# Regrouping the softmax denominator matmuls and double-buffering the sign staging of a binarized weight, in a fused attention and linear kernel

## The chip, the cores and the metric

The kernel runs on the 8 cores of one Trainium2 chip. Each core computes one element of the batch of 8, with its own copy of all weights, and no core talks to another. The metric is the device time in microseconds of the slowest core; the profile is that of the slowest core of one profiled execution. A comparison of two kernels here tells about 2% from no change.

## What is computed

Per batch element, with x of 2048 x 2048 in float32, 16 heads of size 128:

```
def _L0_attn_ref(x, W_Q, W_K, W_V, W_O, b_Q, b_K, b_V, b_O):
    q = einsum('bpd,hde->bphe', x, W_Q) + b_Q          # k, v likewise
    scores = einsum('bqhe,bkhe->bhqk', q, k) / ATTN_SCALE
    scores = where(causal, scores, IGNORE)
    attn = softmax(scores, axis=-1)
    z = einsum('bkhe,bhqk->bqhe', v, attn)
    return einsum('bqhe,hed->bqd', z, W_O) + b_O

def _L0_ffn_ref(x, weight, bias):
    alpha = mean(abs(weight), axis=1, keepdims=True)
    bw = where(weight >= 0, 1.0, -1.0) * alpha
    return einsum('bsi,oi->bso', x, bw) + bias

x = x + _layernorm(_L0_attn_ref(_layernorm(x), ...))
x = x + _layernorm(_L0_ffn_ref(_layernorm(x), weight, bias))
```

## The kernel before, in words

The program is written out by hand for five engines. `p.op(engine, ..., wait=[...], inc=...)` appends one instruction to that engine's list, with the semaphore counts it waits for. Each engine runs its own list strictly in order, so an instruction that waits holds up all that stands behind it in the same list. DMAs are issued from the lists of `sync` (SP) and `gpsimd` (POOL). Nothing is scheduled by a tool: the order of the Python calls is the order on each engine.

There are three stages.

1. First layernorm and transposes of x into `arena_a`, with the projections of head 0 (to about 220 us of the span).
2. The 16 heads, about 130 us each. Per head: the K projection (`emit_w_mms`, 64 matmuls of 512 columns into psD, psE, psC), the V projection (64, into psA and psB), a bound on the scores (`emit_mh_sq`, `emit_mh_mms`, `emit_mh_tail`, `emit_mb`) that becomes `mbias`, and 16 transposes of V. Then come four query groups g = 0 to 3 of 512 queries. Group g has 4(g+1) key chunks of 128 keys. The Q projection of the next head (64 matmuls, psA and psB) is issued behind the last group's denominators.
3. The binarized weight is made (`emit_bw_tile`, 16 tiles of 128 rows), and then 16 row tiles of x run through the output projection (`emit_front_pe`, L759), layernorm, transposes and the second linear layer (L868), and the last layernorm.

**One query group.** For each key chunk j, TensorE makes the scores transposed (`emit_score`, L569, one matmul of 512 columns) in one of four PSUM halves: chunks 0, 1 in psA, 2, 3 in psB, 4, 5 in psA again, and so on. ScalarE turns a pair of chunks into exponentials with one instruction over 1024 columns (`emit_exp`, L583), written to `ptil`. A score matmul waits until the exponential that last read its half is done. The last four chunks of a group stand on the causal diagonal: POOL zeroes the part left of it (L593) and multiplies the diagonal block with a triangle (L596), both in `emit_mask`. The denominators (`emit_den`, L608) are matmuls of an all-ones matrix with each chunk, summed in psC. A denominator matmul waits for the chunk's exponential, or for its mask. Then ScalarE computes the reciprocal as Ln (L637) and Exp (L641), VectorE multiplies every chunk by it (L651), and TensorE multiplies with V (L669) into psE. The scores of the first four chunks of the next group are issued before these L669 matmuls; their exponentials overwrite `ptil` and wait for L669 to have read it.

**What sets the order.** In the kernel before, `emit_emd` emits for each pair an exponential, the masks, and the two denominator matmuls; only then are the next two scores emitted:

```
for j in range(min(4, nchunks), nchunks):
    emit_score(g + 1, j, pe_sc)
    if (j + 1) % estep == 0 and j + 1 > 4:
        emit_emd(g + 1, j + 1 - estep, pe_sc, sc_exp, gp_mask_j)
```

**The binarized weight.** For tile t: POOL loads 128 rows of the weight (L408, 1 MB, two buffers `fwst`), VectorE sums the absolute values (L411) and scales the sum (L415), ScalarE writes the sign into `v_sb` (L421), VectorE multiplies by alpha (L425), TensorE transposes 16 blocks into psD and psE (L438), ScalarE copies both into `arena_a` (L444). There is one staging buffer, `v_sb`, so the sign of tile t+1 waits for the transposes of tile t; it also stands behind the copies of tile t in ScalarE's list. After tile 4, `emit_front_pe(0)` puts the first output projection on TensorE. `emit_front_pe(i)` first issues, from SP, the load of the attention output z of row tile i (L741, 512 KB, into `qt_sb` for even i and `kt_sb` for odd i) and of the x rows (L747).

Of the kernel before, what the change touches and what calls it, by code (L numbers as in the profile page):

```python
# [10 lines left out]
ALU = mybir.AluOpType  # L11
# [49 lines left out]
def build_program(SEQ, DM, H):  # L61
# [252 lines left out]
    pe_bw_last = 0  # L314

# [84 lines left out]

    def emit_bw_tile(t):
        nonlocal pe_bw_last
        fpar = t % 2
        wait = [("SC", sc_ln1t_all),
# [13 lines left out]
        w2 = [(FWs[fpar], fw_t), ("PE", pe_bw_last)]  # L418
        if t == 0:
            w2.append(("PE", pe_av_all[H - 1]))  # L420
        sc_sign_d[t] = p.op("scalar", lambda e, fpar=fpar: e.activation(  # L421
            v_sb[:], fwst[fpar], AF.Sign, bias=0.0, scale=1.0),
            wait=w2, inc="SC",
            lowp="binarized weight is a bf16 matmul operand")
        dv_bw = p.op("vector", lambda e: e.tensor_scalar(  # L425
            v_sb[:], v_sb[:], twoal[:, 0:1], None, ALU.mult),
# [3 lines left out]
        for half in range(2 if NCH > 1 else 1):  # L430
# [5 lines left out]
            for c in range(c0, c1):  # L436
                w3 = wait if c == c0 else ()
                tgt = p.op("tensor", lambda e, c=c, b=b, c0=c0: e.transpose(  # L438
                    b[:, (c - c0) * 128:(c - c0 + 1) * 128],
                    v_sb[:, c * 128:(c + 1) * 128],  # L440
                    eye_sb[:]), wait=w3, inc="PE" if c == c1 - 1 else None)
            pe_bw_last = tgt
            sc_bw_evac_half[half] = p.op(
                "scalar", lambda e, t=t, b=b, c0=c0, c1=c1: e.copy(  # L444
                    bwt3[:, c0:c1, t * 128:(t + 1) * 128],
                    b[:, 0:(c1 - c0) * 128].rearrange("p (c q) -> p c q",
                                                      c=c1 - c0)),
                wait=[("PE", pe_bw_last)], inc="SC")
# [72 lines left out]
    for h in range(H):  # L521
# [68 lines left out]
        def emit_mask(g, j, sc_exp, gp_mask_j):  # L590
            r = j - g * TPG
            if r > 0:
                p.op("gpsimd", lambda e, j=j, r=r: e.memset(  # L593
                    ptil[:, j * GQ:j * GQ + r * 128], 0.0),
                    wait=[("SC", sc_exp[j])], inc="GP")
            gp_mask_j[j] = p.op("gpsimd", lambda e, j=j, r=r: e.tensor_tensor(  # L596
                ptil[:, j * GQ + r * 128:j * GQ + (r + 1) * 128],
                ptil[:, j * GQ + r * 128:j * GQ + (r + 1) * 128],
                tri_sb[:], ALU.mult), wait=[("SC", sc_exp[j])], inc="GP")

        def emit_den(g, j, sc_exp, gp_mask_j):
            chunks = (g + 1) * TPG
            wait = [("SC", sc_exp[j])] if j < g * TPG else \
                [("GP", gp_mask_j[j])]
            if j == 0:
                wait.append(("SC", sc_rinv_prev))
            pe_den_d[g] = p.op("tensor", lambda e, j=j, chunks=chunks:
                               e.matmul(psC[:, 512:512 + GQ], onem_sb[:],  # L608
                                        pslot[j], start=(j == 0),
                                        stop=(j == chunks - 1)),  # L610
                               wait=wait,
                               inc="PE" if j == chunks - 1 else None)

        def emit_emd(g, j0, pe_sc, sc_exp, gp_mask_j):
            emit_exp(g, j0, pe_sc, sc_exp)
            for jj in range(j0, j0 + estep):
                if jj >= g * TPG:
                    emit_mask(g, jj, sc_exp, gp_mask_j)
                emit_den(g, jj, sc_exp, gp_mask_j)
# [383 lines left out]
```

How the kernel before makes its waits and increments, by code:

```python
        def thunk(e, fn=fn, wait=wait, inc=inc, incn=incn, lowp=lowp):  # L43
            for (s, v) in wait:
                e.wait_ge(sems[s][0], v)
            if lowp is not None:
                with nc.allow_low_precision(reason=lowp):
                    ins = fn(e)
            else:
                ins = fn(e)
            if inc is not None:
                ins.then_inc(sems[inc][0], incn)
```

## Time and profile before

| | us |
|---|---|
| median of 3 runs | 2859.36 |
| lowest and highest of these | 2858.36, 3082.75 |
| the profiled execution | 2857.58 |
| its span on the slowest core (core 7) | 2856.1 |
| spans of the 8 cores | 2848.7 to 2856.1 |
| mean granted TensorE clock of the cores | 0.806 to 0.810 of full speed |

The span runs from the first to the last instruction of a core; the profiled execution's time is 1.5 us longer. Engines are PE (TensorE matmuls), PEld (its weight loads), DVE (VectorE), ACT (ScalarE), POOL (GpSimd), and SP, which issues DMAs. A row of the timeline gives a start, a duration, engine, line, output and inputs, and in brackets how long the engine had sat idle before and what ended that.

### The profile page before, as it was taken

The page shows a single profiled execution, that of the slowest core. Times are in us where ns is not written, and L with a number is a line of the kernel's source. Part 1 is how long each engine was busy: PE and PEld are TensorE (multiplying, and loading weights), DVE is VectorE, ACT ScalarE, POOL GpSimd, SP SyncE. Part 2 cuts the span into 40 slices and gives each one's busy share as a digit, 9 for nine tenths or more (in the row PEclk, how much of TensorE's full clock was granted, in tenths as well). Part 3 has the DMA queues.
Part 4 walks back from the last instruction along what each step waited for, and adds up shares of the span by engine and source line. Part 5 has one row for each costly group of instructions (what it writes and reads, how often), then busy time and mean ns, then how long its engine had stood idle before and what let it go on. Part 6 is the DMA issues. An engine that isn't in the chain of part 4 may idle for free.

```text
span 2856.1 us, 27277 instructions; the slowest of 8 cores (2848.7 to 2856.1 us)
## 1 busy us (share of the span) xinstructions
PE 2027.9 (71%) x8336; PEld 827.4 (29%) x8336; DVE 937.5 (33%) x1696; ACT 629.9 (22%) x785; POOL 239.3 (8%) x558
## 2 busy tenths in 40 slices
PE   2556776858586776768586766768585549999995
PEld 1222222313132322323131322223131224444442
DVE  3432322223132222222232322222231445555554
ACT  1222122130303122121303121221303451111111
POOL 0001001010101000110101011011101000000000
PEclk9667877878686878778686878778786669999998
DMA  6410110202021110102021113122110522223221
GB/s 142 125 17 12 19 21 12 26 6 25 6 24 13 19 21 12 19 11 26 6 24 14 19 13 49 19 41 28 34 32 6 187 103 74 74 74 106 79 74 59
DMA packets 178474, 119.33 MB, mean 42 GB/s; under 512 B 168100, under 2 KB 168100, under 8 KB 170148
## 3 DMA queue, kind: packets, MB, share of 16 engines
q0 software_dynamic: 107200, 75.51, 14.6%
q1 hardware_dynamic: 71140, 42.07, 5.8%
q8 instruction: 79, 1.29, 0.2%
q14 instruction: 55, 0.45, 0.1%
HBM read 125.97 MB, written 25.17 MB: 53 GB/s over the span
## 4 chain that ended last, share of the span: by engine, by line
PE 62%; ACT 14%; issue 8%; DVE 8%; POOL 4%; DMA 2%; DVEq 1%; ACTq 1%; POOLq 0%
ACT ptil L583 10%; PE psA L362 8%; PE psB L362 8%; PE psC L608 7%; PE psE L669 5%; PE psC L362 4%; PE psA L759 4%; PE psC L868 4%; PE psB L759 4%; PE psB L569 3%; PE psA L569 3%; POOL ptil L596 2%; PE psD L868 2%; PE psE L868 2%; DVE ptil L651 2%
## 5 line engine op out<-in xcount | busy, mean ns | idle before, releaser
L608 PE MATMUL psC<-ptil,onem_sb 128*128 128x512 bf16 x640 | 274.2, 491 | 459.9 <-ACT ptil L583 165.3
L651 DVE TENSOR_TENSOR ptil<-ptil,c 128x512 bf16<-128x512 bf16 x640 | 220.4, 421 | 918.7 <-ACT c L641 918.7
L362 PE MATMUL psA<-arena_a,wbuf 128*128 128x512 bf16 x1024 | 319.7, 400 | 3.1 <-ACT arena_a L276 3.1
L362 PE MATMUL psB<-arena_a,wbuf 128*128 128x512 bf16 x1024 | 318.5, 399 | 2.8 <-ACT arena_a L276 2.8
L608 PEld LDWEIGHTS psC<-ptil,onem_sb 128*128 128x128 bf16 x640 | 63.9, 100 | 687.0 <-issue 675.8
L583 ACT ACTIVATE ptil<-psA,mbias 128x1024 bf16<-128x1024 f32 x160 | 178.1, 1113 | 343.4 <-PE psA L569 181.1
L583 ACT ACTIVATE ptil<-psB,mbias 128x1024 bf16<-128x1024 f32 x160 | 177.8, 1111 | 254.8 <-PE psB L569 254.8
L669 PE MATMUL psE<-ptil,v 128*128 128x512 bf16 x640 | 189.0, 430 | 28.6 <-DVE ptil L651 28.6
L596 POOL TENSOR_TENSOR ptil<-ptil,tri_sb 128x128 bf16<-128x128 bf16 x256 | 108.5, 424 | 1145.9 <-ACT ptil L583 1145.8
L487 ACT ACTIVATE srow<-srow 1x1 f32<-1x1 f32 x32 | 6.5, 202 | 843.9 <-DVE srow L482 843.9
L868 PE MATMUL psC<-arena_a,c 128*128 128x512 bf16 x512 | 153.1, 381 | 17.3 <-DVE c L852 17.3
L569 PE MATMUL psA<-qt,kt 128*128 128x512 bf16 x320 | 143.0, 542 | 27.1 <-DVE v L557 27.1
L362 PE MATMUL psC<-arena_a,wbuf 128*128 128x512 bf16 x544 | 157.2, 379 | 4.5 <-DVE qt L376 4.5
L569 PE MATMUL psB<-qt,kt 128*128 128x512 bf16 x320 | 147.2, 556 | 0.0
L362 PEld LDWEIGHTS psB<-arena_a,wbuf 128*128 128x128 bf16 x1024 | 104.7, 102 | 137.5 <-issue 28.9
L362 PEld LDWEIGHTS psA<-arena_a,wbuf 128*128 128x128 bf16 x1024 | 104.0, 102 | 139.5 <-issue 31.1
L669 PEld LDWEIGHTS psE<-ptil,v 128*128 128x128 bf16 x640 | 64.3, 101 | 176.2 <-issue 140.9
L868 PE MATMUL psD<-arena_a,c 128*128 128x512 bf16 x256 | 97.5, 381 | 0.0
L868 PE MATMUL psE<-arena_a,c 128*128 128x512 bf16 x256 | 97.3, 380 | 0.0
L362 PE MATMUL psD<-arena_a,wbuf 128*128 128x512 bf16 x240 | 90.9, 379 | 4.3 <-issue 3.4
L362 PE MATMUL psE<-arena_a,wbuf 128*128 128x512 bf16 x240 | 90.9, 379 | 0.0
L759 PE MATMUL psA<-arena_b,kt 128*128 128x512 bf16 x256 | 77.1, 383 | 3.4 <-ACT c L782 3.4
(124 smaller groups left out, 2082.4 us busy)
## 6 DMA issues: line engine op xcount, KB each, us to landing
c<-fw POOLq DMA_DIRECT2D x16, 1024.0 KB, 6.4
ptil<-x SPq DMA_DIRECT2D x16, 1024.0 KB, 6.9
out<-wbuf POOLq DMA_DIRECT2D x16, 1024.0 KB, 9.4
wbuf<-wq POOLq DMA_DIRECT2D x16, 512.0 KB, 6.4
wbuf<-wk POOLq DMA_DIRECT2D x16, 512.0 KB, 6.3
c<-x SPq DMA_DIRECT2D x8, 1024.0 KB, 5.9
wbuf<-wv POOLq DMA_DIRECT2D x16, 512.0 KB, 6.3
zs<-c SPq DMA_DIRECT2D x64, 128.0 KB, 2.0
```

The source lines that it names most:

```text
L362: e.matmul(banks[bidx], wslot[sl][:, c * 128:(c + 1) * 128], ln1t3[:, c, s * SLW:(s + 1) * SLW], start=(c == 0), stop=(c == NCH - 1)),
L487: t_ln = p.op("scalar", lambda e, wh=which: e.activation(srow[0:1, 18 + wh:19 + wh], srow[0:1, 16 + wh:17 + wh], AF.Ln, bias=0.0, scale=1. ...
L569: pe_sc[j] = p.op("tensor", lambda e, j=j, g=g, hb=hb: e.matmul(schalf[hb], kt_sb[:, j * 128:(j + 1) * 128], qt_sb[:, g * GQ:(g + 1) * GQ] ...
L583: t_exp = p.op("scalar", lambda e, buf=buf, dst=dst: e.activation(dst, buf, AF.Exp, bias=mbias[:, 0:1], scale=C_ATTN), wait=wait, inc="SC")
L596: gp_mask_j[j] = p.op("gpsimd", lambda e, j=j, r=r: e.tensor_tensor(ptil[:, j * GQ + r * 128:j * GQ + (r + 1) * 128], ptil[:, j * GQ + r * ...
L608: e.matmul(psC[:, 512:512 + GQ], onem_sb[:], pslot[j], start=(j == 0), stop=(j == chunks - 1)),
L651: dv_norm[j] = p.op("vector", lambda e, j=j, g=g: e.tensor_tensor(pslot[j], pslot[j], rbc[g % 2], ALU.mult), wait=wait, inc="DV")
L669: pe_av = p.op("tensor", lambda e, j=j, chunks=chunks: e.matmul(psE[:, 0:GQ], v_sb[:, j * 128:(j + 1) * 128], pslot[j], start=(j == 0), st ...
L759: p.op("tensor", lambda e, hh=hh, s=s, d=zrd: e.matmul(projb[s], d[:, hh * 128:(hh + 1) * 128], Bz[:, hh * DM + s * 512:hh * DM + s * 512 ...
L868: p.op("tensor", lambda e, c=c, s=s: e.matmul(ffnb[s], ln3t[:, c * 128:(c + 1) * 128], bwt3[:, c, s * 512:s * 512 + PSW], start=(c == 0), ...
```

## The change

It has two parts.

**Denominators and masks.** `emit_mask`, `emit_den` and `emit_emd` are gone. The loop over a group's pairs emits only scores and exponentials. At the head of the loop body for group g, all four masks are emitted, then all 4(g+1) denominator matmuls in a row, and then Ln and Exp as before. The number of instructions stays the same. POOL's and ScalarE's lists keep their order in this stage; only TensorE's changes.

```
-                emit_emd(0, j + 1 - estep, pe_sc, sc_exp, gp_mask_j)
+                emit_exp(0, j + 1 - estep, pe_sc, sc_exp)
         for g in range(NG):
             chunks = (g + 1) * TPG
-            pe_den = pe_den_d[g]
+            gp_mask_j = {}
+            for r in range(TPG):
+                j = g * TPG + r
...
+            pe_den = 0
+            for j in range(chunks):
+                wait = [("SC", sc_exp[j])] if j < g * TPG else \
+                    [("GP", gp_mask_j[j])]
+                if j == 0:
+                    wait.append(("SC", sc_rinv_prev))
+                pe_den = p.op("tensor", lambda e, j=j, chunks=chunks: e.matmul(
+                    psC[:, 512:512 + GQ], onem_sb[:], pslot[j],
+                    start=(j == 0), stop=(j == chunks - 1)),
+                    wait=wait, inc="PE" if j == chunks - 1 else None)
             p.drain("scalar")
...
                 for j0 in range(0, min(4, nchunks), estep):
-                    emit_emd(g + 1, j0, pe_sc, sc_exp, gp_mask_j)
+                    emit_exp(g + 1, j0, pe_sc, sc_exp)
                 for j in range(min(4, nchunks), nchunks):
                     emit_score(g + 1, j, pe_sc)
                     if (j + 1) % estep == 0 and j + 1 > 4:
-                        emit_emd(g + 1, j + 1 - estep, pe_sc, sc_exp,
-                                 gp_mask_j)
+                        emit_exp(g + 1, j + 1 - estep, pe_sc, sc_exp)
```

TensorE's list of the kernel before from the L669 matmuls of group 0 to those of group 1 (psA and psB take scores, psC denominators, psE the product with V):

```order
L669 MATMUL psE<-ptil,v 128x512 x4
L608 MATMUL psC<-ptil,onem_sb 128x512 x4
L569 MATMUL psA<-qt,kt 128x512 x2
L608 MATMUL psC<-ptil,onem_sb 128x512 x2
L569 MATMUL psB<-qt,kt 128x512 x2
L608 MATMUL psC<-ptil,onem_sb 128x512 x2
L569 MATMUL psA<-qt,kt 128x512 x2
L569 MATMUL psB<-qt,kt 128x512 x2
L669 MATMUL psE<-ptil,v 128x512 x8
```

The same stretch of the changed kernel, whose lines are L585 for scores, L635 for denominators and L672 for the product with V:

```order
L672 MATMUL psE<-ptil,v 128x512 x4
L585 MATMUL psA<-qt,kt 128x512 x2
L585 MATMUL psB<-qt,kt 128x512 x2
L635 MATMUL psC<-ptil,onem_sb 128x512 x8
L585 MATMUL psA<-qt,kt 128x512 x2
L585 MATMUL psB<-qt,kt 128x512 x2
L672 MATMUL psE<-ptil,v 128x512 x8
```

The eight denominators of group 1, which stood as four, two and two ahead of and between the score pairs, now stand in one block behind all of the group's scores. In groups 2 and 3 the block has 12 and 16.

**Binarized weight.** The sign goes to `v_sb` for even tiles and to `kt_sb` for odd ones, and waits for the transposes two tiles back. The copies out of psD and psE are emitted by a function of their own, `emit_bw_evacs`, behind the sign of the next tile.

```
+        stg = (v_sb, kt_sb)[fpar]
...
-        w2 = [(FWs[fpar], fw_t), ("PE", pe_bw_last)]
-        if t == 0:
+        w2 = [(FWs[fpar], fw_t), ("PE", pe_bw_par[fpar])]
+        if t < 2:
             w2.append(("PE", pe_av_all[H - 1]))
...
+        if t >= 1:
+            emit_bw_evacs(t - 1)
...
+        if i == 1:
+            wait.append(("PE", B_PE))
```

The last two lines are in `emit_front_pe`: since `kt_sb` now stages signs, the z load of row tile 1 waits for `B_PE`, the count of TensorE at the end of the transposes of tile 15. Behind it in SP's list stand the load of x rows 1 and the z load of row tile 2.

ScalarE's list of the kernel before at the start of the binarized weight (v and kt are the staging buffers, c holds the weight rows):

```order
L421 ACTIVATE v<-c 128x2048
L444 COPY arena_a<-psD 128x8x128
L444 COPY arena_a<-psE 128x8x128
L421 ACTIVATE v<-c 128x2048
L444 COPY arena_a<-psD 128x8x128
L444 COPY arena_a<-psE 128x8x128
```

And of the changed kernel, where L438 is the sign and L410 the copy:

```order
L438 ACTIVATE v<-c 128x2048
L438 ACTIVATE kt<-c 128x2048
L410 COPY arena_a<-psD 128x8x128
L410 COPY arena_a<-psE 128x8x128
L438 ACTIVATE v<-c 128x2048
L410 COPY arena_a<-psD 128x8x128
L410 COPY arena_a<-psE 128x8x128
L438 ACTIVATE kt<-c 128x2048
```

The sign of tile 1 now stands ahead of the copies of tile 0, and so on to the end, where the copies of tile 15 stand alone.

## Rows read from the trace of the kernel before

**Rows 1.** Page: the chain that ended last, share of the span by line

```profile
ACT ptil L583 10%; PE psA L362 8%; PE psB L362 8%; PE psC L608 7%; PE psE L669 5%; PE psC L362 4%; PE psA L759 4%; PE psC L868 4%; PE psB L759 4%; PE psB L569 3%; PE psA L569 3%; POOL ptil L596 2%; PE psD L868 2%; PE psE L868 2%; DVE ptil L651 2%
```

**Rows 2.** Groups of instructions: count | busy us, mean ns | idle before, releasers

```profile
L608 PE MATMUL psC<-ptil,onem_sb 128*128 128x512 bf16 x640 | 274.2, 491 | 459.9 <-ACT ptil L583 165.3 <-POOL ptil L596 158.8 <-POOL ptil L593 135.8
L583 ACT ACTIVATE ptil<-psA,mbias 128x1024 bf16<-128x1024 f32 x160 | 178.1, 1113 | 343.4 <-PE psA L569 181.1 <-DVE mbias L517 69.0 <-DVE ptil L651 58.7
```

**Rows 3.** Timeline of one head, groups 0 to 2: exponentials and one denominator row

```profile
1107.45 1.11 ACT L583 ACTIVATE ptil<-psA,mbias 128x1024 bf16<-128x1024 f32 x1 [4.30 <-DVE mbias L517]
...
1111.46 1.11 ACT L583 ACTIVATE ptil<-psB,mbias 128x1024 bf16<-128x1024 f32 x1 [2.89 <-PE psB L569]
...
1118.21 1.11 ACT L583 ACTIVATE ptil<-psA,mbias 128x1024 bf16<-128x1024 f32 x1 [1.96 <-PE psE L669]
...
1119.22 1.11 ACT L583 ACTIVATE ptil<-psB,mbias 128x1024 bf16<-128x1024 f32 x1
...
1125.07 1.11 ACT L583 ACTIVATE ptil<-psB,mbias 128x1024 bf16<-128x1024 f32 x1 [2.26 <-PE psB L569]
...
1133.19 0.59 PE L608 MATMUL psC<-ptil,onem_sb 128*128 128x512 bf16 x2
...
1145.14 1.11 ACT L583 ACTIVATE ptil<-psB,mbias 128x1024 bf16<-128x1024 f32 x1 [2.89 <-PE psB L569]
```

**Rows 4.** Timeline of the same head, group 3, to the next projection (L362)

```profile
1154.63 1.02 PE L608 MATMUL psC<-ptil,onem_sb 128*128 128x512 bf16 x4
...
1155.49 0.59 PE L569 MATMUL psA<-qt,kt 128*128 128x512 bf16 x2
...
1156.30 1.11 ACT L583 ACTIVATE ptil<-psA,mbias 128x1024 bf16<-128x1024 f32 x1 [2.29 <-PE psA L569]
...
1157.55 0.59 PE L608 MATMUL psC<-ptil,onem_sb 128*128 128x512 bf16 x2 [1.47 <-ACT ptil L583]
...
1160.85 1.06 PE L569 MATMUL psA<-qt,kt 128*128 128x512 bf16 x2
...
1162.12 1.11 ACT L583 ACTIVATE ptil<-psA,mbias 128x1024 bf16<-128x1024 f32 x1 [2.22 <-PE psA L569]
...
1172.78 1.11 ACT L583 ACTIVATE ptil<-psB,mbias 128x1024 bf16<-128x1024 f32 x1 [2.89 <-PE psB L569]
...
1175.02 0.42 POOL L596 TENSOR_TENSOR ptil<-ptil,tri_sb 128x128 bf16<-128x128 bf16 x1
...
1176.14 1.01 PE L362 MATMUL psA<-arena_a,wbuf 128*128 128x512 bf16 x2
```

**Rows 5.** Windows: stretch, length, busy us (count) by engine, granted clock, DMA share, GB/s

```profile
1118.20:1125.00 6.80, 3.22 (x12) 0.95 (x10) 0.69 (x1) 3.23 (x3) 0.95 (x3) 1.00 0.08 19
...
1159.10:1176.00 16.90, 8.56 (x18) 2.20 (x18) 0.00 (x0) 5.25 (x5) 2.95 (x8) 0.50 0.00 0
...
2345.00:2800.00 455.00, 445.73 (x2205) 201.58 (x2204) 249.40 (x362) 82.79 (x160) 7.46 (x14) 1.00 0.28 80
```

**Rows 6.** Timeline of the binarized weight and of the hand-over to row tile 1

```profile
2271.63 1.01 ACT L444 COPY arena_a<-psD 128x1024 bf16<-128x1024 bf16 x1 [14.51 <-PE psD L438]
...
2304.06 1.92 ACT L421 ACTIVATE v<-c 128x2048 bf16<-128x2048 f32 x1
...
2308.37 1.01 ACT L444 COPY arena_a<-psD 128x1024 bf16<-128x1024 bf16 x1 [2.39 <-PE psD L438]
...
2310.18 1.92 ACT L421 ACTIVATE v<-c 128x2048 bf16<-128x2048 f32 x1
...
2332.57 1.06 PE L438 MATMUL psE<-eye_sb,v 128*128 128x128 bf16 x8
...
2337.05 1.01 PE L759 MATMUL psA<-arena_b,kt 128*128 128x512 bf16 x2 [3.42 <-ACT c L782]
```

**Rows 7.** Weight-row loads (L408), all 16: time from issue to landing

```profile
DMA to landing us min/median/max: 5.1/6.4/10.4
```

**Rows 8.** Loads of z (L741), all 16: time from issue to landing

```profile
DMA to landing us min/median/max: 4.4/10.7/12.8
```

More of the change, by code:

```diff
@@ L314, in build_program @@
     pe_bw_last = 0
+    pe_bw_par = [0, 0]
+    pe_bw_tr = {}
     def emit_w_mms(h, wi, only_slice=None):
@@ L399, in build_program, with emit_bw_evacs @@
     sc_ln1t_all = sc_evacA[NT - 1]
+    def emit_bw_evacs(t):
+        hn2 = max(NCH // 2, 1)
+        for half in range(2 if NCH > 1 else 1):
+            b = (psD_bf, psE_bf)[half]
+            c0 = half * hn2
+            c1 = NCH if half else hn2
+            sc_bw_evac_half[half] = p.op(
+                "scalar", lambda e, t=t, b=b, c0=c0, c1=c1: e.copy(
+                    bwt3[:, c0:c1, t * 128:(t + 1) * 128],
+                    b[:, 0:(c1 - c0) * 128].rearrange("p (c q) -> p c q",
+                                                      c=c1 - c0)),
+                wait=[("PE", pe_bw_tr[(t, half)])], inc="SC")
     def emit_bw_tile(t):
@@ L417, in emit_bw_tile @@
         dv_fw_free[t] = dv_as
-        w2 = [(FWs[fpar], fw_t), ("PE", pe_bw_last)]
-        if t == 0:
+        w2 = [(FWs[fpar], fw_t), ("PE", pe_bw_par[fpar])]
+        if t < 2:
             w2.append(("PE", pe_av_all[H - 1]))
[L421 to L426, printed above, removed]
+        sc_sign_d[t] = p.op("scalar", lambda e, fpar=fpar, stg=stg:
+                            e.activation(stg[:], fwst[fpar], AF.Sign,
+                                         bias=0.0, scale=1.0),
+                            wait=w2, inc="SC",
+                            lowp="binarized weight is a bf16 matmul operand")
+        if t >= 1:
+            emit_bw_evacs(t - 1)
+        dv_bw = p.op("vector", lambda e, stg=stg: e.tensor_scalar(
+            stg[:], stg[:], twoal[:, 0:1], None, ALU.mult),
             wait=[("SC", sc_sign_d[t]), ("DV", dv_al)], inc="DV",
@@ L437, in emit_bw_tile @@
                 w3 = wait if c == c0 else ()
[L438 to L441, printed above, removed]
-            pe_bw_last = tgt
[L443 to L448, printed above, removed]
+                tgt = p.op("tensor", lambda e, c=c, b=b, c0=c0, stg=stg:
+                           e.transpose(b[:, (c - c0) * 128:(c - c0 + 1) * 128],
+                                       stg[:, c * 128:(c + 1) * 128],
+                                       eye_sb[:]), wait=w3,
+                           inc="PE" if c == c1 - 1 else None)
+            pe_bw_tr[(t, half)] = tgt
+            pe_bw_last = tgt
+        pe_bw_par[fpar] = pe_bw_last
     def emit_mh_sq(which, h):
@@ L588, in emit_exp @@
                 psbuf_last_rd[jj % 4] = t_exp
[L590 to L619, printed above, removed]
         pe_sc = {}
         sc_exp = {}
-        gp_mask_j = {}
-        pe_den_d = {}
         mb_done = False
@@ L931, in build_program @@
             emit_front_pe(0)
+    emit_bw_evacs(NT - 1)
     B_PE = p.cnt("PE")
```

9 lines of the change are left out of this document (8 added, 1 removed).

## The prediction

> **What bounds the kernel now.** I began with the chain of waits on the page. It is spread over many lines, but one pair of lines stands out: the exponentials of ScalarE are its largest entry and the denominator matmuls its fourth [rows 1]. Both belong to the heads stage, which is 16 times some 130 us. Then I read the groups of instructions. The denominators have 274 us of busy time and 460 us of idle time before them, all of it waiting for an exponential or a mask. The exponentials out of psA sat idle for 343 us, 181 of them waiting for scores [rows 2]. So neither engine is full: each waits for the other. The timeline shows why. In group 3 the order is denominators, scores, exponential, and the next denominators start 0.14 us behind the end of that exponential (1156.30 + 1.11 = 1157.41, then 1157.55) [rows 4]. The next scores stand behind them in the list. A pair therefore costs exponential, 0.14, two denominators, two scores and a step of about 0.22, one after another, although the four score halves would let ScalarE run ahead. Where the scores are there, two exponentials start 1.01 us apart [rows 3].
>
> **Unit prices.** Full clock: four denominators take 1155.49 - 1154.63 = 0.86, so 0.215 each; two scores take 0.59 to their end, and the exponential starts 0.22 later. Half clock: two scores take 1.06, the exponential starts 0.21 later [rows 4], and I take 0.43 for one matmul, twice 0.215.
>
> **The change, part one: denominators.** Nothing is added or removed, 640 matmuls move. A score pair no longer waits for the previous pair's exponential, only for the one two pairs back. So two buffers share the cycle of exponential, wait, scores, step: (1.11 + 0.14 + 0.59 + 0.22) / 2 = 1.03 us a pair at full clock, (1.11 + 0.14 + 1.06 + 0.21) / 2 = 1.26 at half. The pair cost 1.11 + 0.14 + 0.43 + 0.59 + 0.22 = 2.49 at full, and 3.32 at half with 0.86 for two denominators. The end of a group stays: from the start of the last exponential over its masks to the last denominator is 1176.14 - 1172.78 = 3.36, in which the last mask ends 2.66 behind that start [rows 4]. Unless the block of denominators ends later, the gain of a group is how much earlier its last exponential starts.
>
> - Group 0: the second exponential follows the first at 1107.45 + 1.01 = 1108.46 in place of 1111.46 [rows 3]: 3.0.
> - Group 1: the first exponential ends at 1119.32, scores from 1119.46, third exponential at 1120.27. The second ends at 1120.33, so the fourth starts at 1120.33 + 0.14 + 0.59 + 0.22 = 1121.28, in place of 1125.07 [rows 3]: 3.8 (at half clock 1121.74: 3.3).
> - Group 2: TensorE is free at 1133.19. Third exponential at 1134.00, three pairs later 1137.09, in place of 1145.14 [rows 3]: 8.1. The eight denominators without a mask end by 1138.6, ahead of the last mask (1139.75), so the end of 3.36 holds.
> - Group 3: TensorE is free at 1154.63, third exponential at 1155.44, the last at 1160.59; the last scores are issued by 1160.37. Here the block decides: 16 x 0.215 = 3.44 ends at 1163.81, just behind masks (1163.62), in place of 1176.14 [rows 4]: 12.3.
>
> That is 27.2 us a head, 435 us in 16. At half clock all the way: in group 2 the last scores are in at 1138.03 and 12 x 0.43 ends at 1143.19, against 1145.14 + 3.36 = 1148.50: 5.3. In group 3 the scores are in at 1161.99 and 16 x 0.43 ends at 1168.87: 7.3. With 3.0 and 3.3 this is 18.9 a head, 302 in all. These are the two ends for the clock. I take the full one. The stretch 1118.20 to 1125.00 had PE busy 3.22 of 6.80 us and kept 1.00; the stretch at 0.50, 1159.10 to 1176.00, had about the same share (8.56 of 16.90), but part of that is the doubled time of matmuls at half clock [rows 5]. The new score phase has 0.43 us of matmul pitch in 1.03, comes straight out of L669 matmuls, and ends in a dense block. Group 0 I left at half. Two small things cancel as far as I can see: the pauses for Ln, Exp and the first L651 may now and then drop the clock, and the Q projection, which starts at half clock now (two matmuls in 1.01 against 0.59) [rows 4], would start at full.
>
> The Trainium skill's page "TensorE: Matmul & The Clock Gate", section "HAM oscillation", says that pauses of TensorE between bursts put the clock back to half, again and again; by that rule, taken strictly, the sum would be the 302 and not the 435. The stretch at 1.00 with 3.22 of 6.80 us busy speaks against the strict reading [rows 5]. The same page, section "Seeing it yourself", states a limiter that lowers the clock of a die "once three cores of a die run dense matmuls", which a denser program would meet more. The trace does not agree: with all eight cores in the same code, 445.73 of 455.00 us were busy and the granted clock was 1.00 [rows 5].
>
> What stands behind the moved work: the Q projection of the next head comes directly behind the block in group 3, and hides Ln, Exp and L651 as before. POOL's masks and ScalarE's list are unchanged in order, and the weight loads on POOL's queue have a whole head to land.
>
> **Part two: binarized weight.** A tile takes 2310.18 - 2304.06 = 6.12 us: sign 1.92, then ScalarE idle 2.39 until psD is transposed, then two copies [rows 6]. With the next sign in that pause, the pitch is 6.12 - 1.92 = 4.20, with 0.47 of idle time left. Next in line are the loads: two buffers, each held for landing and sign, (6.4 + 1.9) / 2 = 4.2 at the median, but (10.4 + 1.9) / 2 = 6.2 at the slowest [rows 7, 6], which is no gain. I take 4.4 for the ten tiles behind the first output projection: 10 x 1.7 = 17. For the five ahead of it, where the loads crowd, I take 4. The stall of 14.51 us for that projection [rows 6] stays but for its earlier start. So 21, bounds 0 and 15 x 1.92 = 29.
>
> The new wait costs. z of row tile 1 is now loaded only when tile 15 is transposed. Before, L759 for it started 2337.05 - 2333.63 = 3.4 us behind that point, held by ScalarE's copies [rows 6]. A z load takes 4.4 to 12.8, median 10.7 [rows 8]. Cost 10.7 - 3.4 = 7, bounds 1 and 9; TensorE's list is what waits, and all later row tiles stand behind. Net for part two: 14, from -9 to 28.
>
> **Sum.** 2857.6 (the profiled execution; the median of the runs is 1.8 higher) - 435 - 14 = 2408 us.
>
> **Rivals.**
> - The clock falls to half in the score phases. For it: the long stretches at 0.50 in today's phases [rows 5]. Against: as above. 2857.6 - 302 - 14 = 2542.
> - The scores don't run ahead: if the half is really released only with the next exponential, a pair costs 2.06 and only the denominators leave it. Gains: 1.5, 2.7, 5.0, 7.0, so 16.2 a head, 259 in all: 2585. Against: the wait in the code is for the last reader of the half alone.
> - Slower: denser work on eight cores takes the projections down to half clock. A head has 192 projection matmuls, each 0.215 dearer at half. The gain of 27.2 is gone at 127 of them, and 2% slower (57 us, 3.6 a head) begins at 143. All 192, with the attention also at half, give 2857.6 + 16 x (41.3 - 18.9) - 14 = 3202. Against: 1.00 over 455 dense us [rows 5].
> - Part one does nothing because something I don't see paces the groups: within 2%, about 2844. The idle times in rows 2 say otherwise.
>
> **How the numbers follow.** Forecast 0.80, half clock 0.12, scores not ahead 0.04, nothing 0.02, slower 0.02. About 2% is what a measurement tells from no change, so faster 0.96, same 0.02, slower 0.02. The low end has part two at its best (28) and a Q projection that starts at full clock; if eight of its matmuls are at half now, that is 1.7 a head: 2857.6 - 435 - 28 - 26 = 2369. The high end, 2490, is 70 towards the half-clock case with part two at nothing; it leaves out that case itself and those beyond, 0.2 together. Range 2370 to 2490.
>
> **What would show it.** Exponentials in group 3 should start 1.0 to 1.1 us apart, and their idle time out of psA should fall from 343 us to below 150. The denominators should appear as a block with a pitch of 0.215, mean near 0.38 or less by the profile's way of counting, and idle time below 100 us. A head should take about 103 us. In the binarized weight signs should be 4.2 to 4.8 us apart, and TensorE should wait about 10 us for a DMA ahead of row tile 1. Wrong would be: exponentials 2 us apart, a granted clock of 0.50 through group 3, or a block of denominators at 0.43 each.

## The result, and the profile after

The changed kernel takes 2375.68 us at the median of 10 runs (lowest 2372.78), against 2863.7 for the kernel before (10 runs, lowest 2855.46). The ratio is 0.8313, with a 95% interval from 0.8293 to 0.8333: 17% faster. Most kernels here also have some longer runs, in which the cores of one die show a lower granted clock: they are in the medians (and raise that of `diagfirst` by some 57 us), but not in the ratios and traces. The forecast was 2408 with a range from 2370 to 2490, so the time lies inside it, but 32 us below the forecast and only 6 above the low end.

The profiled execution took 2376.52 us, its slowest core 2374.9. The page, with the busy times, the granted clock in 40 slices and the chain of waits that answers to [rows 1]:

```profile
PE 1874.9 (79%) x8336; PEld 803.6 (34%) x8336; DVE 938.1 (40%) x1696; ACT 613.6 (26%) x785; POOL 240.2 (10%) x558
...
PEclk9768988989889898898989989898886899999997
...
PE psA L364 10%; PE psB L364 9%; PE psE L672 8%; ACT ptil L599 6%; PE psC L364 5%; PE psC L871 5%; PE psA L762 5%; PE psB L762 5%; PE psC L635 3%; POOL ptil L625 3%; PE psE L871 2%; PE psD L871 2%; PE psD L364 2%; PE psE L364 2%; DMA c<-x 2%
```

The clock row of the kernel before:

```profile
PEclk9667877878686878778686878778786669999998
```

The same 8336 matmuls, but the exponentials are down from 10% to 6% of the chain and the denominators from 7% to 3%. The clock row reads 8 and 9 through the heads, where before it was 6 to 8: its mean over the cores rose from 0.808 to 0.911. The groups that answer to [rows 2], L635 being the denominators and L599 the exponentials:

```profile
L635 PE MATMUL psC<-ptil,onem_sb 128*128 128x512 bf16 x640 | 182.6, 399 | 52.1 <-POOL ptil L622 25.2 <-POOL ptil L625 22.9
L599 ACT ACTIVATE ptil<-psA,mbias 128x1024 bf16<-128x1024 f32 x160 | 178.1, 1113 | 183.3 <-PE psE L672 78.0 <-DVE mbias L533 69.1 <-PE psA L585 35.8
L599 ACT ACTIVATE ptil<-psB,mbias 128x1024 bf16<-128x1024 f32 x160 | 177.0, 1106 | 0.0
```

And of the kernel before, the exponentials out of psB:

```profile
L583 ACT ACTIVATE ptil<-psB,mbias 128x1024 bf16<-128x1024 f32 x160 | 177.8, 1111 | 254.8 <-PE psB L569 254.8
```

The denominators lost 408 of their 460 us of idle time, and 92 us of busy time besides: far fewer of them run at half clock (a mean of 399 ns in place of 491), and in a block the next one starts before the last has ended (16 take 3.62 us, where one alone is shown with 0.38), so that in the kernel `diagfirst` below, with the same mean but no block of 16, they are busy for 213 us and not for 183. The exponentials took the same 178.1 us. Out of psA their waits for scores fell from 181 us to 36, out of psB from 255 to nothing.

**Group 3 of one head**, to hold beside [rows 4]: scores are L585, denominators L635, the last mask L625, Ln L640.

```profile
935.99 0.59 PE L585 MATMUL psA<-qt,kt 128*128 128x512 bf16 x2
...
936.78 1.11 ACT L599 ACTIVATE ptil<-psA,mbias 128x1024 bf16<-128x1024 f32 x1 [1.78 <-PE psA L585]
937.80 1.10 ACT L599 ACTIVATE ptil<-psB,mbias 128x1024 bf16<-128x1024 f32 x1
938.04 0.59 PE L585 MATMUL psA<-qt,kt 128*128 128x512 bf16 x2 [1.03 <-ACT ptil L599]
938.84 1.11 ACT L599 ACTIVATE ptil<-psA,mbias 128x1024 bf16<-128x1024 f32 x1
...
941.11 0.59 PE L585 MATMUL psB<-qt,kt 128*128 128x512 bf16 x2 [0.41 <-ACT ptil L599]
...
941.53 3.62 PE L635 MATMUL psC<-ptil,onem_sb 128*128 128x512 bf16 x16
941.91 1.11 ACT L599 ACTIVATE ptil<-psB,mbias 128x1024 bf16<-128x1024 f32 x1
...
944.15 0.43 POOL L625 TENSOR_TENSOR ptil<-ptil,tri_sb 128x128 bf16<-128x128 bf16 x1
...
945.25 0.58 ACT L640 ACTIVATE psC<-psC 128x512 f32<-128x512 f32 x1 [2.23 <-PE psC L635]
```

The exponentials start 1.02 and 1.04 us apart, and behind the first one without any idle time. The scores at 938.04 wait only for the exponential that frees their half, which ends at 936.78 + 1.11 = 937.89, and not for the one of the pair before them, which runs to 938.90. All 16 denominators follow as one block. The group runs from its first exponential to Ln in 945.25 - 936.78 = 8.5 us. The windows of group 1 of the same head, of that score phase, and of 440 us of the last stage, with the columns of [rows 5]:

```profile
911.00:918.20 7.20, 4.84 (x17) 1.61 (x17) 1.68 (x4) 4.18 (x4) 2.39 (x7) 1.00 0.08 18
935.90:941.50 5.60, 3.28 (x13) 1.18 (x13) 0.69 (x1) 4.71 (x5) 0.00 (x0) 1.00 0.10 23
1860.00:2300.00 440.00, 431.34 (x2129) 194.69 (x2127) 238.21 (x342) 79.59 (x154) 6.93 (x13) 1.00 0.28 78
```

The score phase (second row) has PE busy 3.28 of 5.60 us and keeps a granted clock of 1.00. The last stage is as dense as before and also at 1.00.

**By stage**, means over the 8 cores, taken from the traces of the two profiled executions:

| | before | after |
|---|---|---|
| one head (between the mbias instructions of neighbouring heads) | 129.67 | 100.76 |
| last matmul of the product with V of head 15, its start | 2217.0 | 1756.3 |
| from there to the output projection of row tile 1 | 115.8 | 91.7 |
| of that, from the last transposes of tile 15 | 3.8 | 5.3 |
| from there to the end | 519.9 | 520.4 |

Heads 460.7, weight stage 24.1, the rest -0.5: together 484.3 us on the mean core. The forecast had 435, 14 and 0.

### The profile page after: what moved, and what is told of

Read it like the earlier page. It is cut to its first block, busy times and chain, and to the rows that moved or that the text cites. A ratio compares the mean times of both kernels' runs of the same rounds, so it can differ in the third digit from the quotient of the medians.

```text
span 2374.9 us, 27278 instructions; the slowest of 8 cores (2362.5 to 2374.9 us)
## 1 busy us (share of the span) xinstructions
PE 1874.9 (79%) x8336; PEld 803.6 (34%) x8336; DVE 938.1 (40%) x1696; ACT 613.6 (26%) x785; POOL 240.2 (10%) x558
## 4 chain that ended last, share of the span: by engine, by line
PE 65%; ACT 9%; DVE 8%; issue 8%; POOL 4%; DMA 3%; DVEq 2%; ACTq 0%; POOLq 0%; SPq 0%
PE psA L364 10%; PE psB L364 9%; PE psE L672 8%; ACT ptil L599 6%; PE psC L364 5%; PE psC L871 5%; PE psA L762 5%; PE psB L762 5%; PE psC L635 3%; POOL ptil L625 3%; PE psE L871 2%; PE psD L871 2%; PE psD L364 2%; PE psE L364 2%; DMA c<-x 2%
## 5 line engine op out<-in xcount | busy, mean ns | idle before, releaser
L654 DVE TENSOR_TENSOR ptil<-ptil,c 128x512 bf16<-128x512 bf16 x640 | 220.4, 420 | 479.3 <-ACT c L644 479.3
L364 PE MATMUL psA<-arena_a,wbuf 128*128 128x512 bf16 x1024 | 304.2, 384 | 5.1 <-ACT arena_a L276 3.1
L364 PE MATMUL psB<-arena_a,wbuf 128*128 128x512 bf16 x1024 | 303.9, 384 | 2.8 <-ACT arena_a L276 2.8
L672 PE MATMUL psE<-ptil,v 128*128 128x512 bf16 x640 | 188.1, 390 | 51.8 <-DVE ptil L654 51.8
L599 ACT ACTIVATE ptil<-psA,mbias 128x1024 bf16<-128x1024 f32 x160 | 178.1, 1113 | 183.3 <-PE psE L672 78.0
L635 PE MATMUL psC<-ptil,onem_sb 128*128 128x512 bf16 x640 | 182.6, 399 | 52.1 <-POOL ptil L622 25.2
L625 POOL TENSOR_TENSOR ptil<-ptil,tri_sb 128x128 bf16<-128x128 bf16 x256 | 108.6, 424 | 890.3 <-ACT ptil L599 890.3
L599 ACT ACTIVATE ptil<-psB,mbias 128x1024 bf16<-128x1024 f32 x160 | 177.0, 1106 | 0.0
L585 PE MATMUL psA<-qt,kt 128*128 128x512 bf16 x320 | 109.5, 427 | 78.1 <-ACT ptil L599 50.8
L364 PEld LDWEIGHTS psA<-arena_a,wbuf 128*128 128x128 bf16 x1024 | 101.0, 99 | 131.2 <-issue 16.3
L585 PE MATMUL psB<-qt,kt 128*128 128x512 bf16 x320 | 109.0, 426 | 25.9 <-ACT ptil L599 25.9
L672 PEld LDWEIGHTS psE<-ptil,v 128*128 128x128 bf16 x640 | 62.3, 97 | 187.3 <-issue 152.3
L635 PEld LDWEIGHTS psC<-ptil,onem_sb 128*128 128x128 bf16 x640 | 62.5, 98 | 174.2 <-issue 125.0
L221 ACT ACTIVATE rstd<-mv,epsb_sb 128x1 f32<-128x1 f32 x64 | 18.9, 295 | 262.4 <-DVE mv L213 221.8
```

The costliest lines, as they stand in the source:

```text
L221: p.op("scalar", lambda e, pr=par: e.activation(rstd[pr][:], mv2[pr][:, 1:2], AF.Ln, bias=epsb_sb[:, 0:1], scale=1.0), wait=w)
L364: e.matmul(banks[bidx], wslot[sl][:, c * 128:(c + 1) * 128], ln1t3[:, c, s * SLW:(s + 1) * SLW], start=(c == 0), stop=(c == NCH - 1)),
L585: pe_sc[j] = p.op("tensor", lambda e, j=j, g=g, hb=hb: e.matmul(schalf[hb], kt_sb[:, j * 128:(j + 1) * 128], qt_sb[:, g * GQ:(g + 1) * GQ] ...
L599: t_exp = p.op("scalar", lambda e, buf=buf, dst=dst: e.activation(dst, buf, AF.Exp, bias=mbias[:, 0:1], scale=C_ATTN), wait=wait, inc="SC")
L635: pe_den = p.op("tensor", lambda e, j=j, chunks=chunks: e.matmul(psC[:, 512:512 + GQ], onem_sb[:], pslot[j], start=(j == 0), stop=(j == ch ...
L654: dv_norm[j] = p.op("vector", lambda e, j=j, g=g: e.tensor_tensor(pslot[j], pslot[j], rbc[g % 2], ALU.mult), wait=wait, inc="DV")
```

## The experiments

None of the eight kernels leaves out any part of the computation. The lines in their profiles are those of their own text, so the same instruction can have another line number.

**Each part by itself.** `p1_only` is the kernel before with the changed attention code (denominators in a block), `p2_only` is the kernel before with the changed binarized weight and its z wait.

> Only part one (denominators and masks regrouped), the binarized weight as before. My theory: the heads shrink by 29.0 us each (the last L669 matmul ends 463 us earlier in the trace of the changed kernel), and part two is worth some 19 us, so 2857 - 463 = 2394 us. Rival: the two parts help each other (a denser end of the heads brings the weight stage forward at a better clock), then part one alone gives less, 2410 or more.

> Only part two (signs double-buffered, copies behind the next sign, z of row tile 1 loaded late). My theory: 19 us less than before, 2838 us, in the weight stage alone. Rival, that the late z load eats most of it and the gain of that stage in the changed kernel came from elsewhere: 2850 or more.

Measured: p1_only 2398.07 us (ratio 0.8382, 0.8361 to 0.8402), p2_only 2835.84 (ratio 0.9911, 0.9879 to 0.9943), with the kernel before at 2859.05 beside them. Gains of 461.0 and 23.2, in sum 484.2, against 483.4 for both together (2859.05 - 2375.68). The parts add, and each is near its expectation (2394 and 2838). Part two alone is less than the 2% that a comparison can tell; its gain is read from the traces. In p1_only a head takes 100.77 us and the weight stage 116.2, in p2_only 129.55 and 91.7: each part acts in its own stage alone. 95% of the gain is part one.

**What in part one does it?** Two things moved at once: the scores run ahead of the exponentials, and the denominators no longer stand between them. `serial` keeps the block of denominators and takes the running ahead away, by a wait for the previous pair's exponential in `emit_score`:

```
+            if j % 2 == 0 and j >= (2 if g == 0 else 4):
+                wait.append(("SC", sc_exp[j - 1]))
```

> The changed kernel with one wait more: the scores of a pair also wait for the exponential of the pair right ahead, so the two PSUM buffers no longer overlap, but the denominators stay out of the loop. My theory: pairs 2.06 us apart in place of 1.03, which is 1 interval in group 1, 3 in group 2, 5 in group 3 and 1.5 us in group 0, 10.8 us a head, 172 us in all: about 2548 us. Rival, that taking the denominators out of the loop is what pays and the overlap of buffers little: below 2420 us.

Measured: 2675.96 us (2 runs), ratio 0.9354 (0.9322 to 0.9386). A head takes 119.36 us against 100.76, so the running ahead is worth 18.6 us a head, 300 of the 461 us; the other 10.3 a head stay without it. The expectation priced the running ahead at 10.8 a head, and its time was 128 us too low. The rival, below 2420, fell. The timeline of group 3 on its slowest core (exponentials L601, denominators L637) says why, and the window of the same stretch (us, then PE, PEld, DVE, ACT and POOL busy, granted clock, DMA share, GB/s):

```profile
1314.17 1.11 ACT L601 ACTIVATE ptil<-psA,mbias 128x1024 bf16<-128x1024 f32 x1 [1.79 <-PE psA L587]
...
1316.22 1.11 ACT L601 ACTIVATE ptil<-psB,mbias 128x1024 bf16<-128x1024 f32 x1 [0.94 <-PE psB L587]
...
1318.70 1.11 ACT L601 ACTIVATE ptil<-psA,mbias 128x1024 bf16<-128x1024 f32 x1 [1.36 <-PE psA L587]
...
1321.18 1.11 ACT L601 ACTIVATE ptil<-psB,mbias 128x1024 bf16<-128x1024 f32 x1 [1.36 <-PE psB L587]
...
1325.72 5.79 PE L637 MATMUL psC<-ptil,onem_sb 128*128 128x512 bf16 x16
```

```profile
1313.40:1332.00 18.60, 11.28 (x33) 3.71 (x33) 0.69 (x1) 7.08 (x7) 3.52 (x8) 0.63 0.05 8
```

The first pair comes 2.05 us after the one before, as worked out for full clock (1.11 + 0.14 + 0.59 + 0.22 = 2.06). Then the clock falls, the pairs are 2.48 apart, and the block of 16 takes 5.79 us where the changed kernel's took 3.62. The mean clock of the kernel is 0.836 where the changed kernel has 0.911. Not all of the missing 7.8 us a head is the clock: the expectation left out that the third exponential of a group comes later too (on the mean 2.44 us behind the second in place of 1.07 in group 1, 2.05 in place of 1.54 in group 2), 1.9 us a head. But from the last exponential to Ln, where the waits are the same, it is 4.56 and 5.69 us in groups 2 and 3 in place of 3.29 and 3.35, 3.6 a head. So the running ahead pays twice: once for the waits, and once because with scores 1.03 us apart the clock stayed up, and with scores 2.05 apart it fell. The Trainium skill's page "TensorE: Matmul & The Clock Gate", section "HAM oscillation", describes such a loss, again and again, in a kernel whose bursts of matmuls are parted by waits for DMAs; this trace, whose waits are for ScalarE, agrees in kind, with 0.63 granted over the stretch, and the changed kernel's score phase, with pauses of 0.41 to 1.03 us and 1.00 granted, is a case in which the pauses cost nothing.

`diagdefer` is the other half: the kernel before puts denominators of all earlier chunks back between the pairs, and only the four masked ones of a group go to its end (`emit_emd` and its helpers come back into the changed kernel, with this branch):

```
+                if jj >= g * TPG:
+                    emit_mask(g, jj, sc_exp, gp_mask_j)
+                else:
+                    emit_den(g, jj, sc_exp, gp_mask_j)
...
+            for jj in range(g * TPG, chunks):
+                emit_den(g, jj, sc_exp, gp_mask_j)
```

> The changed kernel's weight stage, with the attention order of before except that the four denominators of the diagonal chunks, which wait for masks, stand behind all scores of their group; the others stay between the score pairs. My theory (every denominator in the loop couples the pairs, masked or not): gains of 3.0, 2.4, 2.8 and 2.8 us a head, 11 in all, 176 us and 19 for part two: about 2662 us. Rival, that the masks on POOL are the cost in the loop (half of the denominators' idle time names POOL): 2540 us or less.

Measured: 2621.76 us (3 runs), ratio 0.9163 (0.9133 to 0.9192). A head takes 116.25 us; moving only the masked denominators gives 13.4 a head, 215 in all, where 11 was expected, and 15.5 stay lost. The time lies 40 us below the expected 2662 and 82 above the rival's 2540. The groups of instructions:

```profile
L624 PE MATMUL psC<-ptil,onem_sb 128*128 128x512 bf16 x633 | 246.7, 456 | 288.7 <-ACT ptil L599 153.2 <-POOL ptil L609 94.2 <-POOL ptil L612 36.5
L599 ACT ACTIVATE ptil<-psA,mbias 128x1024 bf16<-128x1024 f32 x160 | 178.1, 1113 | 322.7 <-PE psA L585 164.7 <-PE psE L688 74.0 <-DVE mbias L533 68.9
```

The exponentials' wait for scores is back at 164.7 us (181.1 before), and the denominators' wait for exponentials at 153.2 (165.3 before). So the plain denominators, each behind the exponential of its own pair and ahead of the next scores, chain the two engines without any mask. The masked ones, with POOL's time in the chain as well, cost nearly as much in the loop: 13.4 of the 28.9 us a head.

**Is a block needed?** If the fault is only that a denominator waits for the newest exponential, it may stand between the scores as long as it lags. In `lag2` the denominators of a pair come two pairs later, and the last four at the end:

```
+                        emit_den(g + 1, j - 5, sc_exp, gp_mask_j)
+                        emit_den(g + 1, j - 4, sc_exp, gp_mask_j)
+                for jj in range(nchunks - 4, nchunks):
+                    emit_den(g + 1, jj, sc_exp, gp_mask_j)
```

> The changed kernel, but the denominators go back between the score pairs, two pairs behind: scores of pair k, then denominators of pair k-2, which wait for the same exponential as those scores. No block of 16. My theory (what cost was the wait of the scores behind the denominators of the pair just ahead, not the interleaving): as the changed kernel, 2365 to 2385 us, clock 0.91. Rival (one dense block of matmuls is what keeps the clock at 2.4 GHz): granted clock below 0.88 and 2420 us or more.

Measured: 2391.42 us (4 runs), ratio 0.8366 (0.8349 to 0.8383), with the kernel before at 2860.35 beside it. It is 16 us slower than the changed kernel, less than a comparison can tell, and 6 above the upper end of what was expected, but 29 below the rival. Its cores have 0.896 to 0.912 where the rival had below 0.88. The answers on the cores and two windows of its slowest core, with the product of V (L687) in the second:

```profile
core 1: 2368.3 us, clock 0.912
...
core 5: 2388.9 us, clock 0.896
```

```profile
1427.40:1434.20 6.80, 4.67 (x15) 1.28 (x13) 2.12 (x5) 4.65 (x5) 1.02 (x4) 0.83 0.08 19
1434.30:1441.00 6.70, 5.14 (x14) 1.60 (x15) 2.77 (x8) 2.74 (x4) 1.27 (x4) 0.67 0.00 0
```

```profile
1438.34 3.57 PE L687 MATMUL psE<-ptil,v 128*128 128x512 bf16 x8 [0.84 <-DVE ptil L669]
```

Core 1 keeps 0.912 and takes 2368.3 us, what the changed kernel's cores take (2362.5 to 2374.9). Core 5 has heads in which the clock falls in group 1, as here to 0.67, and the eight matmuls take 3.57 us in place of 2.62. In nine of its 16 heads they take more than 3 us, and these heads last 102.4 us, the others 101.0; on core 1 it happens in none. So the order is as good as the block where the clock holds, and most of the loss is that of such falls, nine times 1.4 us on core 5. Why this order loses the clock in some heads and the block does not was not tried.

**The new wait of part two.** `zbuf` stages the odd signs in a free part of ptil in place of kt_sb, so that the z load of row tile 1 need not wait for tile 15 (the x load behind it does, since its target lies there). The wait that goes stands at the z load, the one that comes at the x load:

```
-        stg = (v_sb, kt_sb)[fpar]
+        stg = (v_sb, ptil[:, 2 * DM:3 * DM])[fpar]
...
-        if i == 1:
-            wait.append(("PE", B_PE))
...
+        if i == 1:
+            wait.append(("PE", B_PE))
```

> The changed kernel, but the odd signs go into the half of ptil that later takes x of row tile 1, so z of row tile 1 is loaded early again and x of row tile 1 late. My theory: TensorE's wait of 6.5 us for the z load ahead of row tile 1 is replaced by the 3.4 us for ScalarE's copies, so 3 us less, 2373 us. As my prediction sized it: 7 us less, 2369 us. Rival, the late x load now stalls VectorE or TensorE further on: 2376 us or more.

Measured: 2376.34 us (5 runs), ratio 0.8304 (0.8286 to 0.8323). In the traces the wait is gone and its place taken by the old one. Of core 0, the last transposes and the first output projection of row tile 1:

```profile
1850.62 1.06 PE L458 MATMUL psE<-eye_sb,ptil 128*128 128x128 bf16 x8
1855.48 0.63 PE L762 MATMUL psA<-arena_b,kt 128*128 128x512 bf16 x1 [3.80 <-ACT c L785]
```

The stretch from the last transposes is 3.8 us on the mean core, as in the kernel before [rows 6], against 5.3 in the changed kernel. So the wait costs 1.5 us on the mean core, which is less than the time of a run can show, and is read from the traces alone. (In the changed kernel's slowest core it is longer, see below.) The time is no lower than the changed kernel's, where the rival had put it, but not for the rival's reason: from there to the end it is 519.6 us on the mean core against 520.4, so the late load of x stalls nothing. The heads end 1.7 us later than in the changed kernel (1758.0 against 1756.3), though their code is the same, and that makes up for the 1.5.

**Beyond the change.** In the changed kernel a group ends with masks: POOL can start on them only when the diagonal chunks, which come last, are out, and Ln starts 945.25 - 941.91 = 3.3 us behind the start of the last exponential. `diagfirst` starts each group with its diagonal chunks, has the denominators in lag2's order, and keeps zbuf's staging:

```
+        def ck(g, j):
+            return g * TPG + j if j < TPG else j - TPG
...
+            c = ck(g, j)
...
-                schalf[hb], kt_sb[:, j * 128:(j + 1) * 128],
...
+                schalf[hb], kt_sb[:, c * 128:(c + 1) * 128],
...
+                if jj < TPG:
+                    emit_mask(g, jj, sc_exp, gp_mask_j)
...
-                    psE[:, 0:GQ], v_sb[:, j * 128:(j + 1) * 128], pslot[j],
...
+                    psE[:, 0:GQ], v_sb[:, c * 128:(c + 1) * 128], pslot[j],
```

> The kernel zbuf with denominators two pairs behind and with the four diagonal chunks taken first in each group, so that POOL's masks are done while other exponentials run. My theory: the end of a group from the start of the last exponential falls from 3.3 to 1.95 us in groups 1 and 2 and from 3.1 to 1.7 in group 3, 4.0 us a head, 64 us: about 2309 us. Rival, masks were hidden behind the denominator block anyway: 2365 us or more.

Measured: ratio 0.8126 (0.8091 to 0.8161), with 2319.75 us in the profiled execution (5 runs, median 2381.35). The expectation was 2309. A head takes 97.39 us, 3.4 less than in the changed kernel, where 4.0 was expected. The end of a group 3, Ln being L659:

```profile
915.92 1.11 ACT L603 ACTIVATE ptil<-psB,mbias 128x1024 bf16<-128x1024 f32 x1
...
917.17 0.59 PE L628 MATMUL psC<-ptil,onem_sb 128*128 128x512 bf16 x2 [0.41 <-ACT ptil L603]
...
917.86 0.58 ACT L659 ACTIVATE psC<-psC 128x512 f32<-128x512 f32 x1 [0.83 <-PE psC L628]
```

Ln comes 1.94 us behind the start of the last exponential in place of 3.3, and only two denominators are left to do by then. In group 0, where every chunk is on the diagonal, it stays at 3.5.

`evacnorm` goes on from there. The product with V is linear in the probabilities, so the division can be done once, on its result. The L654 multiplications (640 of them) go, the product with V no longer waits for them, and the evacuation of psE multiplies by the reciprocal sums instead of only casting:

```
-            for j in range(chunks):
...
-                dv_norm[j] = p.op("vector", lambda e, j=j, g=g: e.tensor_tensor(
-                    pslot[j], pslot[j], rbc[g % 2], ALU.mult),
...
-                wait = [("DV", dv_norm[j])]
+                wait = []
...
-            wait = [("PE", pe_av), (ZWs[zpar], zw_par_t[zpar])]
-            dv_zevac[gidx] = p.op("vector", lambda e, zpar=zpar: e.tensor_copy(
-                zstage[zpar], psE[:, 0:GQ]), wait=wait, inc="DV")
+            wait = [("PE", pe_av), (ZWs[zpar], zw_par_t[zpar]),
+                    ("SC", sc_rinv)]
+            dv_zevac[gidx] = p.op("vector", lambda e, zpar=zpar, g=g:
+                                  e.tensor_tensor(zstage[zpar], psE[:, 0:GQ],
+                                                  rbc[g % 2], ALU.mult),
+                                  wait=wait, inc="DV")
```

> The kernel diagfirst, but the normalizer is applied once when psE is copied out (one VectorE instruction a group) and not to every chunk of ptil; L672 no longer waits for Ln, Exp and VectorE. My theory: from the start of a group's last exponential to the first of the next 3.15 us in place of 6.1, three times a head, and L672 at 0.215 in place of 0.335 each; with the end of group 3 some 12 us a head, 190 us, less 3 for z: about 2183 us. Rival, ScalarE's Ln and Exp stay in front of the next exponentials and pace it all the same: 2270 us or more.

Measured: 2235.44 us (4 runs), ratio 0.7809 (0.7787 to 0.7832): 22% faster than the kernel before and 6% faster than the changed one, the best version found. The expectation was 2183. A head takes 92.19 us, 8.6 less than in the changed kernel where some 12 were expected, and 5.2 less than in diagfirst. The hand-over into groups 2 and 3 is near what was expected (3.15 us), as here from group 2 into group 3 on its slowest core:

```profile
863.07 1.11 ACT L603 ACTIVATE ptil<-psB,mbias 128x1024 bf16<-128x1024 f32 x1
...
865.01 0.58 ACT L659 ACTIVATE psC<-psC 128x512 f32<-128x512 f32 x1 [0.83 <-PE psC L628]
...
865.64 2.75 PE L683 MATMUL psE<-ptil,v 128*128 128x512 bf16 x12
...
866.34 1.11 ACT L603 ACTIVATE ptil<-psA,mbias 128x1024 bf16<-128x1024 f32 x1
...
869.03 1.11 ACT L603 ACTIVATE ptil<-psA,mbias 128x1024 bf16<-128x1024 f32 x1 [0.58 <-PE psA L589]
```

The next group's first exponential starts 3.27 us behind the last one's start. TensorE goes from scores straight into the product with V, and is done with it 865.64 + 2.75 = 868.4. The third pair of scores stands behind those twelve matmuls, so the exponential at 869.03 waits 0.58 for it: there the group is paced by TensorE and no longer by ScalarE.

What falls short is mostly the hand-over from group 0 into group 1. On the same core:

```profile
844.76 1.11 ACT L603 ACTIVATE ptil<-psB,mbias 128x1024 bf16<-128x1024 f32 x1
...
848.25 0.58 ACT L659 ACTIVATE psC<-psC 128x512 f32<-128x512 f32 x1 [2.38 <-PE psC L628]
...
849.65 1.25 PE L683 MATMUL psE<-ptil,v 128*128 128x512 bf16 x4
...
850.57 1.11 ACT L603 ACTIVATE ptil<-psA,mbias 128x1024 bf16<-128x1024 f32 x1 [1.02 <-PE psE L683]
```

Here all the masks come last, Ln starts 3.5 us behind the last exponential, and the next exponential waits for scores and a product that TensorE can only then begin: 5.8 us. The means over cores and heads are 5.90, 3.28 and 3.29 us for the three hand-overs, where the changed kernel has 6.56, 6.13 and 6.14 and 3.15 was expected of each. So 2.75 us of the missing 3.4 stand at the first one.

## Why the prediction was right

**The mechanism.** The forecast had a pair of chunks going from exponential, denominators, scores, step one after another (2.49 us) to two buffers that share the cycle (1.03). The timeline shows 1.02 and 1.04. Serial and diagdefer show that this is the cause and not a companion of the block: with the block but no running ahead 300 us come back, and with denominators of the newest pair ahead of the next scores 246 do (2621.76 - 2375.68).

**Part one, by groups**, the means over cores and heads of what each group gained, beside the forecast:

| group | forecast | measured |
|---|---|---|
| 0 | 3.0 | 3.0 (7.85 to 4.81) |
| 1 | 3.8 | 4.2 (13.65 to 9.45) |
| 2 | 8.1 | 8.2 (19.99 to 11.79) |
| 3 | 12.3 | 11.9 (27.16 to 15.23) |
| rest of the head | 0 | 1.5 (61.02 to 59.47) |

In brackets is the time from one group's Ln to the next one's (for group 0 from the end of the score bound). The four groups give 27.4 against 27.2. The term that was left out is the last: the Q projection behind the block starts at full clock (945.27, two matmuls in 0.59) where it ran at half [rows 4]. The prediction saw it, put 1.7 a head on it, and used that for the low end only. 16 times 1.5 is 24 of the 26 us by which part one was too small. It is read from the intervals; no run tests it alone, but the traces bear it out. The product with V stands right behind the 64 matmuls of the projection, which began at 1176.14 [rows 4] before; first the row before, then the two of after:

```profile
1191.63 3.62 PE L669 MATMUL psE<-ptil,v 128*128 128x512 bf16 x16
```

```profile
945.27 0.59 PE L364 MATMUL psA<-arena_a,wbuf 128*128 128x512 bf16 x2
...
959.08 3.62 PE L672 MATMUL psE<-ptil,v 128*128 128x512 bf16 x16
```

The 64 matmuls took 1191.63 - 1176.14 = 15.5 us and take 959.08 - 945.27 = 13.8. So the step that failed is the sentence that this term and the pauses for Ln, Exp and L651 cancel.

The sum itself holds but for small slips that change nothing in it: the terms of a pair at half clock give 3.38 and not 3.32 (3.32 is the interval in the trace before, between exponentials at 1162.12 and 1165.44), the masks of group 3 would end at 1160.59 + 2.66 = 1163.25 and not at 1163.62, and 16 times 1.7 at the low end is 27 and not 26.

**The half-clock rival** (2542) did not happen: the clock was 1.00 through the new score phase, with work for TensorE every 1.03 us, as the prediction had argued. Serial bears that out and shows how near the rival lies: with pairs 2.05 us apart the clock does fall. **Scores not ahead** (2585) fell with the first timeline, and serial, which makes it so, costs 300 us more than the changed kernel where the rival put 177 (2585 - 2408): its price was too small, mostly by what the clock gives back. **Slower** (3202) did not appear: 431.34 us were busy in 440 at 1.00, and each of the eight cores had 1.00 in that stretch. The limiter that the Trainium skill's page "TensorE: Matmul & The Clock Gate", section "Seeing it yourself", has for such a load was not met here either. **Nothing** (2844) fell.

**Part two** was mis-sized in both terms, in the same direction. The gain was put at 21 and is 24.1 + 1.5 = 25.6. The weight stage of the slowest core and its hand-over:

```profile
1804.91 0.62 PE L458 MATMUL psD<-eye_sb,kt 128*128 128x128 bf16 x8
...
1806.88 0.61 PE L458 MATMUL psD<-eye_sb,v 128*128 128x128 bf16 x8 [0.91 <-ACT arena_a L410]
...
1845.76 1.01 PE L458 MATMUL psD<-eye_sb,kt 128*128 128x128 bf16 x8 [2.40 <-ACT arena_a L410]
1846.56 1.06 PE L458 MATMUL psE<-eye_sb,kt 128*128 128x128 bf16 x8
...
1854.09 1.01 PE L762 MATMUL psA<-arena_b,kt 128*128 128x512 bf16 x2 [6.47 <-DMA kt<-zs]
```

```profile
1847.70 0.36 SPq L744 DMA_DIRECT2D kt<-zs  x1
```

```profile
DMA to landing us min/median/max: 5.9/10.7/12.1
```

From the transposes of tile 6 to those of tile 15 it is (1845.76 - 1806.88) / 9 = 4.32 us a tile: the forecast 4.4 holds. But tile 6 follows tile 5 by only 1.97 us, since its sign is already staged when the output projection lets TensorE go. That is a second effect of the two buffers. Tiles 5 to 15 took 1845.76 - 1804.91 = 40.85 us here, and on the mean core 39.9 where the kernel before has 60.9: 21 gained where the step that priced ten tiles by the pitch alone had 17. The other 4.6 of the 25.6 lie ahead of the output projection, where 4 was taken.

The wait for z was put at 7 us. It costs 1.5 on the mean core and 3.0 on this one, the slowest (6.47 in place of 3.42 [rows 6]). TensorE does wait for the DMA, but the load landed 5.9 us after its issue at 1847.70, as the shortest of the sixteen, and not after the median of 10.7; on the other seven cores it took 4.1 to 4.5 us. The step that failed is the choice of the row: the near end of the bounds (4.4) was its row. Why this load is faster than most is not shown; that it has only the x load behind it, while the others have neighbours, is a guess. That zbuf brings the 3.80 back shows the price.

Together: 25.7 of the gain that the forecast missed lie in the heads and 10.1 in the weight stage, and both misses go the same way. The upper part of the range, kept for a lower clock, was not needed.

**The signs that were named.** Exponentials 1.0 to 1.1 apart: yes. Denominators as one block, mean 399 ns against 380: nearly; their idle time below 100: 52.1. A head of 103: 100.8. A pitch of 4.2 to 4.8 in the weight stage: 4.3. A wait of about 10 for the DMA: 6.5, and 5.0 on the mean core. Idle time of the exponentials out of psA below 150: no, 183.3. Its largest part, 78.0, is the first exponential of a group that waits for the product with V to release ptil. That wait was there before (1.96 at 1118.21 in [rows 3]), and the change does not touch it. The 343 us less all 181 of waits for scores are 162, so 150 had no working behind it; the slip was to take a part of the other waits for what goes.

## What to carry to other kernels

In an engine's list that is worked off in order, an instruction that waits for the newest result of another engine should not stand ahead of work which could run already. Give it a lag (two pairs in lag2), or put it at the end of the block: here that is 461 us of 2859, without an instruction more or less. When such a change is priced, price the clock with it: running ahead also kept TensorE's clock up (serial lost 18.6 us a head, of which about 13 are waits by the count above). And look at what remains at the ends: masks first, and a division moved behind the matmul that it commutes with, took another 140 us off (2376 to 2235).

## What was not expected of the hardware

- The same scores at a pitch of 1.03 us kept the clock at 1.00 with PE busy 3.28 of 5.60 us, and at 2.05 us lost it within one group, over which 0.63 was granted (serial).
- Cores that run the same program differ in it: lag2's core 1 had a mean clock of 0.912 and its core 5 one of 0.896, 20.6 us apart in span, while the changed kernel's cores lie between 0.910 and 0.913.
- The load of z of row tile 1, with one load behind it, landed in 5.9 us on the slowest core and in 4.1 to 4.5 on the others, where the median of the sixteen is 10.7.
